# Where TensorE reads the eight ends of the experts' runs of blocks in a graph and mixture-of-experts kernel

## The reference, cut to what matters

```python
gate = softmax(xt @ Wg)
topv, topi = top_k(gate, 2)
topv = topv / (sum(topv) + 1e-06)
scores = zeros((T, E)).at[arange(T)[:, None], topi].set(topv)
for e in range(E):                        # E = 8
    h = gelu(xt @ W1[e] + b1[e])          # 512 -> 256
    ye = h @ W2[e] + b2[e]                # 256 -> 512
    out = out + ye * scores[:, e:e + 1]
```

## Time and profile before

| | |
|---|---|
| median of three runs | 630.3 us |
| span of the profiled execution | 644.0 us |
| PE busy | 563.7 us (88%) |
| DVE busy | 466.9 us (72%) |
| ACT busy | 280.9 us (44%) |
| POOL busy | 286.1 us (44%) |
| from the first block's first matmul to the last block's | 449.1 to 620.5 us |

### The profile page before, as it was taken

One profiled execution on the slowest core, in us unless ns is written; L12 is line 12 of the kernel. 1 busy time (PEld: TensorE's weight loads), 2 busy tenths in 40 slices (PEclk: granted clock), 3 DMA queues, 4 the chain that ended last, 5 costly groups with the idle time before them and its releaser, 6 DMA issues.

```text
span 644.0 us, 13546 instructions
## 1 busy us (share of the span) xinstructions
PE 563.7 (88%) x4500; PEld 419.5 (65%) x4501; DVE 466.9 (72%) x979; ACT 280.9 (44%) x539; POOL 286.1 (44%) x237
## 2 busy tenths in 40 slices
PE   5788989999999999999999999814899999999970
PEld 3688979667566666666775665814677776767650
DVE  4777888884689999898987332697886655666562
ACT  3464767332342352235322300551565554555452
POOL 4362322130083363446334432525476666666643
PEclk9999899999999999999999999875999999999995
DMA  8253300300032332422331224955977777777755
GB/s 254 87 141 103 94 1 1 77 1 1 21 110 77 118 115 86 123 101 87 110 96 62 67 82 82 387 165 156 281 132 135 134 137 136 132 133 132 131 86 75
DMA packets 39548, 71.71 MB, mean 111 GB/s; under 512 B 12169, under 2 KB 16409, under 8 KB 38826
## 3 DMA queue, kind: packets, MB, share of 16 engines
q0 software_dynamic: 11328, 25.55, 21.7%
q1 hardware_dynamic: 21327, 31.08, 15.3%
q10 hardware_dynamic: 6834, 14.34, 7.0%
HBM read 43.46 MB, written 29.06 MB: 113 GB/s over the span
## 4 chain that ended last, share of the span: by engine, by line
PE 67%; DVE 18%; ACT 6%; issue 4%; DMA 2%; SPq 0%; DVEq 0%; POOLq 0%; ACTq 0%; POOL 0%; PEldq 0%
PE psum L1539 22%; PE psum L1683 11%; PE psum L1523 8%; PE psum L1693 8%; PE psum L1578 7%; PE psum L1453 7%; ACT he L898 3%; DVE hot_lo L1128 3%; DVE hot_key L1128 3%; DVE he_hi L1374 2%; PE psum L1431 2%; DMA src_i<-in_src 1%; PE psum L1660 1%; DVE stat L941 1%; ACT h L746 1%
## 5 line engine op out<-in xcount | busy, mean ns | idle before, releaser
L1128 DVE TENSOR_TENSOR hot_key<-iota_key,key_w 128x1200 f16<-128x1200 f16 x125 | 107.2, 858 | 27.7 <-PE psum L1523 26.7
L719 ACT ACTIVATE counts<-psum 128x400 bf16<-128x400 f32 x125 | 62.1, 507 | 139.1 <-PE psum L1523 137.7
L1539 PE MATMUL psum<-counts,z_hi 125*128 125x500 bf16 x400 | 101.8, 375 | 2.4 <-ACT h L746 1.7
L658 POOL DMA_INDIRECT out_x<-y,target_i x47 | 76.9, 1637 | 59.7 <-ACT y L889 42.0
L1539 PE MATMUL psum<-counts,z_lo 125*128 125x500 bf16 x400 | 101.5, 377 | 0.0
L1523 PE MATMUL psum<-hot_key,hot_lo 128*128 128x200 f16 x750 | 83.6, 252 | 3.8 <-DVE hot_lo L1128 2.2
L1128 DVE TENSOR_TENSOR hot_lo<-iota_lo,lo_w 128x768 f16<-128x768 f16 x125 | 85.2, 681 | 0.0
L1523 PEld LDWEIGHTS psum<-hot_key,hot_lo 128*128 128x128 f16 x750 | 66.8, 99 | 24.5 <-issue 3.5
L898 ACT ACTIVATE he<-psum,eb_col,up_undo 128x128 f32<-128x128 f32 x94 | 42.6, 457 | 85.4 <-PE psum L1683 50.3
L620 POOL TENSOR_TENSOR xt<-xt_whole,xt 125x512 f16<-125x512 f32 x20 | 50.5, 2527 | 53.9 <-DVE xt L1168 40.7
L1683 PE MATMUL psum<-xT_hi,w_both 128*128 128x128 f16 x704 | 65.3, 222 | 5.4 <-issue 4.5
(11 more groups left out here) (274 smaller groups left out, 1136.8 us busy)
## 6 DMA issues: line engine op xcount, KB each, us to landing
out_x<-x SPq DMA_DIRECT2D x20, 224.0 KB
xt_d<-xt SPq DMA_DIRECT2D x20, 224.0 KB
x_res<-in_x SPq DMA_DIRECT2D x19, 224.0 KB
up_raw<-in_L_ffn_W ACTq DMA_DIRECT2D x8, 512.0 KB, 4.1
up_d<-up_split ACTq DMA_DIRECT2D x8, 512.0 KB
w_both<-up_d SPq DMA_DIRECT2D x8, 512.0 KB, 7.9
w_raw<-in_L_ffn_W SPq DMA_DIRECT2D x8, 512.0 KB, 9.3
W_raw<-in_L_gnn_W ACTq DMA_DIRECT2D x2, 1024.0 KB, 5.6
```

Source lines behind the costliest of these rows:

```text
L658: pool.indirect_dma_start(out=out[:, :], in_=y[:, k % YB], in_offset=None, out_offset=bass.IndirectOffsetOnAxis(ap=target_i[:, k:k + 1], a ...
L719: act.activation(counts[:, it % 2, :, place:place + W], psum[:, WIN + w % 2, 0:MW].rearrange("p (w h) -> p h w", w=W), ACT.Copy).then_inc( ...
L1128: ins = dve.tensor_tensor(hot[:, w % RING].rearrange("p s (n two) -> p s n two", two=2), iota[:].rearrange("p (o n two) -> p o n two", o=1 ...
L1539: ins = mm(psum[:, AGG + c, 0:GN], half[:, t, c * 128:(c + 1) * 128], counts[0:P, g % 2, t], start=(t == 0 and n == 0), stop=(t == T - 1 a ...
```

## The change

The eight reads move from between the experts' loops to a place ahead of the score tables. The waits for TOKENS and BLOCKS move with them. The loops take the ends from eight registers.

```diff
@@ ahead of the score tables
+            pe.wait_ge(S["slots_known"], TOKENS)
+            pe.wait_ge(S["slots_known"], BLOCKS)
+            ends = [pe.value_load(end_i[0:1, e:e + 1], min_val=1, max_val=NB) for e in range(NE)]
             pe.wait_ge(S["slots_known"], SCORE_PARTS)
             for n in range(2 * T):
                 if n == 24:
@@ behind them
             ins.then_inc(S["slots_spread"], 1)
-            pe.wait_ge(S["slots_known"], TOKENS)
-            pe.wait_ge(S["slots_known"], BLOCKS)
             start = 0
-            for e in range(NE):
-                end = pe.value_load(end_i[0:1, e:e + 1], min_val=1, max_val=NB)
+            for e, end in enumerate(ends):
                 pe.wait_ge(S["w_lo_ready"], e + 1)
                 with pe.Fori(start, end) as k:
```

## The result

The changed kernel is faster: 623.63 us median (622.13 to 627.88) against 630.39 us (628.87 to 633.93) for the kernel before beside it, a ratio of 0.9888 with the interval [0.9853, 0.9924]. The forecast was 632.3 us with a range of 629.3 to 634.3, so the sign and the range were both wrong; the gain of 6.8 us is also twice the 3.15 us up to which the forecast called a change "same".

The account below looks back on a forecast made before the run. PE, with 67% of the chain, was taken to bound the kernel. Late tables +4.6, come-back -1.4 and borders -1.2 gave +2.0 us on 630.3, so 632.3 us, range 629.3 to 634.3.

Parts of the forecast that it names:

- the 13.7 us between that span and the median of the runs are in both: Profiled span 644.0 against run median 630.3: difference taken as equal in both kernels, so +2.0 was added to 630.3.
- the head's two terms: Ahead of the block loops: eight reads delay the score tables by 4.6 us, of which 1.4 come back behind them.
- The borders, -1.2: Between experts' loops: removing seven reads gains 1.2 us net of 4.5 gross, since the next block gives most back.
- the blocks behind the borders keep their short form: Rival at the borders: the whole 4.5 us is gained and the reads stay nearly covered; 626.3 us, chance 0.05.
- The reads ahead of the tables, +4.6: Ahead of the score tables: the first eight gathers hold the moved reads, about one per gather; tables 4.6 us late.
- The first rival: Ahead of the tables: gathers do not hold the reads, tables only 0.55 us late; 629.7 us, chance 0.15.
- What comes back behind the tables, -1.4: From last table matmul to DVE's reading of it: 1.67 us lateness shrinks to some 0.3, giving 1.4 us back.
- The clock, 0: Around the first block: PE's clock may rise earlier or later; taken as 0, plus or minus 1 us.
- if something in the blocks that I hold fixed, such as the regular 3.90 us, moves: Sign of a wrong prediction in the block loop: 0.05 us on each of 44 blocks would outweigh the whole change.

Follow-up runs that it names:

- plain stores: Kernel before with each block's results stored to spare rows by a plain DMA instead of the indirect add, gathers kept; 634.44 us against 645.24 on chip B.
- seven early reads: Against the kernel before: seven reads ahead of the score tables, the eighth behind them; 644.28 us (1.0015) on chip C, 644.96 us (0.9989) on D.
- the doubled reads: Kernel before with each border's read done twice, on chip A; 636.07 us, ratio 1.0112.

## Why the prediction was wrong

**The step that failed most is the smallest sentence of it:** "the 13.7 us between that span and the median of the runs are in both". They were not an offset. A run takes about 2 us more than its span, so the profile of before belonged to a run of 646 us, and the timed runs were another form. Without reads at the borders the block loops of chips A and B, first block to last, take 149.62 and 168.81 us, 19.2 us apart: nearly 0.5 us for each of 43 blocks. With them it is 156.41 against 169.74, 13.3 us, since the borders cost 6.8 us on A and 0.9 on B. Every other step priced edits in a form in which the timed runs were not. Of the 8.7 us between the forecast and the measured time, 5.6 lie in the borders' term (-6.8 instead of -1.2) and 2.8 in the head's two terms (+0.4 instead of +3.2).

**The borders, -1.2.** In the form it was read from the term held: -0.9 us by the last block on chip B, with the head's change inside it. In the form that was timed it is -6.8. The reason given, that a border's gap is paid back by a shorter block, was right for the earlier trace rows and is exactly what is missing on chip A: there every block is short already, so nothing can come back. Besides, each border costs more there, 1.05 us on average and not 0.63, since the reads start earlier in a gather and wait longer for it: six of them 0.31 to 0.47 us into it, taking 894 to 998 ns, where in the profile of before seven start at 0.68 to 0.99 and take 408 to 729. The rival "the blocks behind the borders keep their short form" gave 626.3 and a chance of 0.05; it came nearest, partly by luck. The blocks behind the borders do stay short without the gap, but because every block is short there and not by anything at the border; and its time is 2.7 us too high, because it took the gaps of the long form, 4.5 us.

**The reads ahead of the tables, +4.6.** Wrong in mechanism and size. The row showed reads held by later gathers and the step took this over to the first eight gathers. There no read was held, in either form: 294 to 326 ns each in the changed kernel and in every variant of it, one every 0.64 us. Eight take 5.2 us (437.89 to 443.08), and the tables start 0.37 us later than they did (0.43 after the scores instead of 0.06). The first rival (reads free, 0.55 late) had this step right. What separates the first eight gathers from the later ones wasn't found; on POOL's rows both last about 1 us, and with plain stores the later ones still hold reads, so the indirect adds alone are not it.

**What comes back behind the tables, -1.4.** In the short form nothing comes back: from the first table matmul to the first GELU it takes 5.74 us in the changed kernel (443.13 to 448.87) and also in the kernel before on chip A, whose rows are:

```profile
443.47 2.10 PE L1667 MATMUL psum<-token_part,at_row 125*128 125x96 f16 x24 [7.16 <-DVE token_part L1326]
446.22 1.49 PE L1667 MATMUL psum<-token_part,at_row 125*128 125x96 f16 x16
...
447.75 0.21 DVE L1342 TENSOR_SCALAR score_low<-psum 128x48 f32<-128x48 f32 x1 [0.51 <-PE psum L1667]
449.21 0.95 ACT L898 ACTIVATE he<-psum,eb_col,up_undo 128x128 f32<-128x128 f32 x2 [2.57 <-PE psum L1683]
```

It was 7.36 in the earlier trace rows. The lateness that should have come back, a PE signal 1.67 us behind its matmuls beside POOL's last gathers, goes with the long form as the late second GELU does; here it is 0.04 us (446.22 + 1.49 to 447.75). In the long form the scores are read 1.8 to 1.95 us behind the start of the last of the eight gathers, however late the tables are, so the prediction's guess that PE's result waits for the gathers fits; that it is the same hold as in the blocks was not tested. In the long form the term was right as far as it could be tested: of the 0.37 us that the tables are late on chip B, 0.04 are left at the first GELU.

**The clock, 0.** This held. No run shows the plus or minus 1 around it; in its place the runs showed when the granted clock goes from 0.50 to 1.00 and how long the first block takes. In the short form it rises 0.5 to 1.1 us behind the first block's start, with the reads or without them, and the first block takes 3.97 us in both kernels. On chip B it rose 3.5 us behind that start in the kernel before (first block 4.88 us) and ahead of it in the changed one (4.53), but the two first blocks together differ by only 0.15 us. It does not follow the reads: seven early reads have it 0.2 us ahead of that start on C and 3.4 behind it on D.

**Put together.** In the long form the prediction's method, corrected for reads that are not held, gives 0.37 - 0.33 - 1.2, about -1.2 us, and -0.9 was measured. In the short form the sum is +0.4 for the head and -6.8 for the borders, -6.4 by the profiles and -6.8 and -5.6 by the medians of the two comparisons. One slip of addition changed nothing: the terms' ends give 631.45 to 634.35, not 631.2 to 634.2. The list of what would prove it wrong named the right signs ("if something in the blocks that I hold fixed, such as the regular 3.90 us, moves"); it looked for them in the changed kernel, and they stood in the gap between the span and the times before anything was changed.

## What to carry to other kernels

Ahead of any sum, compare the profiled run's own time with the median of the timed runs. Here a run takes about 2 us more than its span, and the profile's span lay 13.7 us over the median: the profile showed a form of the kernel that wasn't the one timed, and a stall of 0.63 us that gave 0.52 back in it cost 1.05 us in full in the other. The eight short reads by PE's sequencer (0.30 us, 0.64 with the check) cost 0.4 us in all where PE waited for DVE's scores anyway, and 1.05 us each between the loops, beside a gather, so it pays to read such loop bounds ahead, in a gap that is known to be as long as the row. A stretch in which a kind of instruction is held is no evidence for another stretch, not even when the same neighbour runs beside it: PE's reads took 347 to 998 ns beside the later gathers and 294 to 326 beside the first eight.

## What the chip showed that was not expected

- The same kernel takes about 630 us on chip A and about 645 on B, C and D. The medians of the kernel before stay within 0.5 us of each other over four sets on the last three. The busy times of DVE, ACT and POOL are the same on A and B within 1 us (467.0 and 468.0, 281.7 and 281.1, 287.6 and 287.3). Chip A was met in one set only, so whether the form belongs to the chip or to something else that was different then is not settled, and why the forms differ is open.
- PE's signal for a block's second half comes 0.23 us after its last matmul is issued on A, with an indirect DMA of POOL started up to 1.2 us before it in 34 to 40 of 44 blocks. On B, C and D it is late: in the median 0.73 us after that matmul with the add started 0.64 us before it, 0.84 us on C with a gather started 0.43 us before it. In both cases that is 1.3 to 1.4 us behind the DMA's start; where the DMA lies 1.25 us or more back, the signal takes 0.23 to 0.33 us there too. The reads at the borders are held on all chips, A included (608 to 998 ns on A, 347 to 763 on B, C and D), so only the signals tell the forms apart. What of the DMA holds them was not tested.
- A read of one integer of `end_i` by PE's sequencer takes 293 to 326 ns where no later gather runs beside it (one of the doubled reads took 370), and read and bounds check together repeat every 0.64 us. Started 0.2 to 1.0 us into one of the later gathers it takes 0.35 to 1.0 us; beside the first eight it takes 294 to 326 ns.
